# Routing of a mixture of experts moved out of its own stage and into the attention beside it

## The chip, the core and the metric

The kernel runs on one core of a Trainium2 chip. The core has a matrix engine (TensorE, PE), a vector engine (VectorE, DVE), a scalar engine (ScalarE, ACT), a general engine (GpSimd, POOL), and a queue engine (SyncE, SP) that issues nearly all transfers. Each runs its own list of instructions in order and waits for the others at semaphores. Sixteen DMA engines move data. The metric is the device time of one execution in microseconds (us), as the median of several runs.

## What is computed

The input x is 4 sequences of 1024 tokens of 256 values. It is normalised to xn; then attention (16 heads of 16, causal, with a linear position bias) and a mixture of 8 experts, two per token, both read xn, and the output is their sum with x.

```python
xn = _layernorm(x)
x = x + attention(xn, Wq, Wk, Wv, Wo, bo) + moe(xn, router_logits, gating, linear, ...)

# in moe: routing
var = mean(square(xn)); router_input = xn * rsqrt(var + 1e-6) * rsqrt(F) * router_scale
logits = router_input @ router_logits            # 8 per token
probs = softmax(logits)
_, choices = approx_max_k(logits, k=2)
weights = probs / sum(probs of the two chosen)
# tokens sorted by expert, two small matrix products per expert, results put back and weighted
```

## The kernel before, in words

The program is a row of blocks; at the end of a block all engines meet, and nobody starts the next before.

- **project**: 8 chunks of 512 tokens. SP loads a chunk of x (two buffers, `x_in`), DVE takes mean and variance, POOL the inverse deviation, DVE writes `xn`, PE transposes it and multiplies it by the weights of q and k (four quads of heads, `qkpsum`) and of v and the router (`vpsum`). ACT, DVE and POOL split q and k into three bfloat16 parts each (`parts`; L383, L359, L361, L312). SP stores xn, the parts and v, v as four DMAs per chunk (L257). The loop is a hardware loop over pairs of chunks.
- **route**: POOL finishes the scale of the router's input (L490, L492) and writes constants and the causal mask (L494 to L512). DVE runs 58 small dependent instructions, each waiting for the one before (`then`): top two experts per token, softmax weights, and the position ("slot") of each token in a list sorted by expert. In between, PE sums up the counts of tokens per expert (L521, L522) and ACT takes one exponential. Meanwhile SP loads the first three quads of heads (`load_quad`, 13 DMAs each).
- **attend**: 16 steps, one for each quad of heads of each sequence. For every quad there are 19 "items": PE multiplies q and k into `mpsum` (two buffers of 1024 columns, L824), DVE takes the row maxima under the mask (L742); the last item turns the maxima into extra rows of q, which SP writes back with one DMA (L668, `mrow_in`). 26 items are worked off before step 0 (the lead); then a step consists of 18 pairs of heads, with one item of a later step beside each pair (`PAIR_ITEMS`). In a pair PE computes scores (`spsum`, L835), ACT their exponentials (`probs`, L784), POOL masks the diagonal blocks (L722), PE multiplies by v (`cpsum`, L855), and ACT takes the sums away (`ctxT`, L798 and L802, once each per step). The order of all this is written out by hand. In every step POOL also writes four columns of the slot map by indirect DMA, after unit 2 (L712), from small copies that SP fetches a step ahead (L672, L673). SP loads the experts' first weights `w_gu` right after the first maxima rows (L680).
- **experts**: SP loads the finished map into `places` (L936); POOL gathers rows of xn by it (L951); PE, ACT and DVE compute; POOL scatters the results.
- **combine**: output projection and the weighted sum.

## Time and profile before

| | |
|---|---|
| median of 3 runs | 939.3 us (938.69 to 1016.51) |
| profiled execution | 941.12 us, of which the trace spans 939.4 us |
| PE busy | 812.5 us (86%) |
| DVE busy | 562.1 us (60%) |
| ACT busy | 483.2 us (51%) |
| POOL busy | 390.0 us (42%) |

How to read it: "busy" counts instructions that compute. In a timeline row the first number is the start in us from the beginning of the span, the second the time that the merged instructions take, then engine, line, operation, what is written and read; in brackets stands how long the engine was idle before and what ended that. SPq is the issue of a DMA, not its transfer. The granted clock of PE is given as a share of 2.4 GHz. Stages by the timeline: project 0 to 110, route 117.7 to 158, attend 158.5 to 628, experts and combine 632 to 939.

### The profile page before, as it was taken

Reading aid. Unit: us, or ns where it says so; the run is one execution under the profiler, and the core shown is the slowest. Engines: PE = TensorE matmul, PEld = TensorE weight load, DVE = VectorE, ACT = ScalarE, POOL = GpSimd, SP = SyncE. Lnnn points to the kernel's source line nnn. Section 1 sums busy time; section 2 is a strip of 40 time slices with the busy share of each in tenths; the row PEclk is TensorE's granted clock in tenths of the full one; section 3 lists DMA queues with packets and bytes.
Section 4 is the critical chain, followed back from the end, with each engine's and each line's share of the span. In section 5 each row is a group of like instructions: output and inputs, shape, how many; then the busy total and the mean of one; then the engine's idle time right before and its main releaser. Section 6 shows DMA issues by size and latency. Waiting matters only on the chain. (4 is left out here: it accounts for less than half of the span.)

```text
span 939.4 us, 17505 instructions
## 1 busy us (share of the span) xinstructions
PE 812.5 (86%) x5618; PEld 426.3 (45%) x5619; DVE 562.1 (60%) x1560; ACT 483.2 (51%) x1011; POOL 390.0 (42%) x456
## 2 busy tenths in 40 slices
PE   5989601799999999999999999856999999999598
PEld 2555400134444444444444444313555656555497
DVE  4767364988888888888888888301222222222177
ACT  2333300067777777777777777852333333333374
POOL 3545340033223233322323332323666666665398
PEclk9999855589999999999999999996999999999799
DMA  4999899295555666555566600009222222222485
GB/s 157 221 263 269 213 107 121 34 253 74 62 61 57 82 81 81 67 62 61 59 82 81 81 3 3 2 6 321 86 84 84 84 84 84 84 85 78 129 245 182
DMA packets 115004, 100.32 MB, mean 107 GB/s; under 512 B 58172, under 2 KB 95676, under 8 KB 114876
## 3 DMA queue, kind: packets, MB, share of 16 engines
q1 hardware_dynamic: 105976, 80.50, 46.9%
q0 software_dynamic: 8960, 18.95, 6.4%
q8 instruction: 37, 0.61, 0.3%
q14 instruction: 31, 0.25, 0.1%
HBM read 63.89 MB, written 35.00 MB: 105 GB/s over the span
## 5 line engine op out<-in xcount | busy, mean ns | idle before, releaser
L784 ACT ACTIVATE probs<-spsum 128x512 f32<-128x512 f32 x576 | 312.1, 604 | 169.6 <-PE spsum L835 163.8
L742 DVE CUSTOM_DVE_ANT_0 junk<-mpsum,mask 128x128 bf16<-128x128 f32 (+7 forms) x512 | 360.0, 754 | 58.5 <-issue 51.7
L824 PE MATMUL mpsum<-ks,qs 102*128 102x512 bf16 (+3 forms) x768 | 183.5, 343 | 45.9 <-DVE cpsum L731 26.3
L722 POOL TENSOR_SCALAR_AFFINE_SELECT probs<-probs 128x512 f32<-128x512 f32 x128 | 78.8, 634 | 340.8 <-ACT probs L784 340.8
L835 PE MATMUL spsum<-qs,ks 105*128 105x512 bf16 (+3 forms) x768 | 199.2, 329 | 10.6 <-ACT probs L784 8.3
L855 PE MATMUL cpsum<-probs,vs 128*17 128x256 f32 (+2 forms) x2560 | 152.7, 360 | 1.5 <-POOL probs L722 0.8
L1037 PE MATMUL gu<-w_gu,xTs 128*128 x288 | 139.2, 607 | 1.7 <-ACT xTs L981 1.7
L1016 DVE COPY hT<-hp 128x256 f32<-128x256 f32 x72 | 30.6, 425 | 167.8 <-PE hp L1044 100.6
L824 PEld LDWEIGHTS mpsum<-ks,qs 102*128 102x128 bf16 x768 | 69.8, 100 | 122.5 <-DVE maxima L742 39.8
L835 PEld LDWEIGHTS spsum<-qs,ks 105*128 105x128 bf16 x768 | 67.1, 97 | 102.9 <-ACT probs L784 52.9
L956 POOL DMA_INDIRECT expert_rows<-y,places x72 | 70.7, 983 | 72.2 <-ACT y L990 42.2
L855 PEld LDWEIGHTS cpsum<-probs,vs 128*17 128x17 f32 x2560 | 59.8, 97 | 77.4 <-issue 36.4
L951 POOL DMA_INDIRECT rows<-xn_rows,places x72 | 69.3, 962 | 34.9 <-issue 20.7
L985 ACT ACTIVATE gate<-gu 128x256 f32<-128x256 f32 x72 | 27.7, 384 | 100.7 <-issue 64.0
L1050 PE MATMUL yp<-w_down,hT 128*128 x288 | 74.2, 380 | 0.4 <-issue 0.4
L1037 PEld LDWEIGHTS gu<-w_gu,xTs 128*128 128x128 f32 x288 | 52.1, 193 | 45.4 <-issue 38.5
L712 POOL DMA_INDIRECT slot_map<-entries_now,slots x64 | 61.8, 966 | 17.2 <-issue 17.2
L417 PE MATMUL qkpsum<-xT,w_qk 128*128 128x512 f32 x128 | 59.8, 612 | 4.4 <-DVE rest L359 3.3
L1014 DVE TENSOR_TENSOR hid<-gu,gate 128x256 f32<-128x256 f32 x72 | 30.2, 420 | 49.3 <-ACT gate L985 49.3
L1050 PEld LDWEIGHTS yp<-w_down,hT 128*128 128x128 f32 x288 | 49.1, 190 | 4.6 <-issue 0.9
L312 POOL TENSOR_TENSOR parts<-rest,parts 128x512 bf16<-128x512 f32 x32 | 37.0, 1157 | 32.0 <-DVE parts L361 32.0
L990 ACT ACTIVATE y<-yp 128x256 f32<-128x256 f32 x72 | 27.7, 384 | 36.2 <-issue 31.8
(124 smaller groups left out, 698.5 us busy)
## 6 DMA issues: line engine op xcount, KB each, us to landing
qk_parts<-parts SPq DMA_DIRECT2D x32, 384.0 KB, 4.4
qs<-qk_parts SPq DMA_DIRECT2D x96, 128.0 KB
ks<-qk_parts SPq DMA_DIRECT2D x96, 128.0 KB
yk<-expert_rows SPq DMA_DIRECT2D x32, 256.0 KB, 3.1
v_rows<-vt SPq DMA_DIRECT2D x32, 136.0 KB, 4.5
vs<-v_rows SPq DMA_DIRECT2D x16, 272.0 KB, 12.0
x_in<-in_x SPq DMA_DIRECT2D x8, 512.0 KB, 6.3
xn_rows<-xn SPq DMA_DIRECT2D x8, 512.0 KB, 5.8
```

The source lines that it names most:

```text
L417: last = pe.matmul(qkpsum[:, q % 2], w_qk[:, dh, q], xT[:, par, dh], start=dh == 0, stop=dh == DH - 1)
L712: pool.indirect_dma_start(scratch["map"], bass.IndirectOffsetOnAxis(ap=slots[:, par, k, i:i + 1].bitcast(U32), axis=0), entries[:, par, k, ...
L722: pool.affine_select(out=part, in_=part, compare_op=ALU.is_ge, fill=0.0, base=0, pattern=[[0, 4], [1, P]], channel_multiplier=-1).then_inc ...
L742: last = dve.tensor_tensor_reduce(junk[:, slot, c:c + w], mpsum[:, slot, c:c + w], keep["mask"][:, S - w:S], 1.0, 3 * NEG, ALU.add, ALU.ma ...
L784: act.activation(probs[:, u % PRING, h], spsum[:, (4 * u + h) % SRING], ACT.Exp, scale=SCALE).then_inc(exp_done, 1)
L824: last = pe.matmul(mpsum[:, slot, at + c:at + e], qs[hq][0:R_MAX, h, qt * P:(qt + 1) * P], ks[hq][0:R_MAX, h, c:e], start=True, stop=True)
L835: last = pe.matmul(spsum[:, (4 * u + h) % SRING, c:c + w], ks[hq][:, h, kt * P:(kt + 1) * P], qs[hq][:, h, q0:q0 + w], start=True, stop=True)
L855: last = pe.matmul(cpsum[32 * h:32 * h + VW, q0 % CH:q0 % CH + w], vs[hq][:, kt, h], probs[:, u % PRING, h, c:c + w], start=i == 0 and (u, ...
L951: pool.indirect_dma_start(rows[:, s % RR], None, scratch["xn"], bass.IndirectOffsetOnAxis(ap=places[:, s, 0:1].bitcast(U32), axis=0)).then ...
L956: pool.indirect_dma_start(scratch["y"], bass.IndirectOffsetOnAxis(ap=places[:, s, 1:2].bitcast(U32), axis=0), y[:, s % RR], None).then_inc ...
L1037: last = pe.matmul(gu[:, par], xT[:, par, dh], w_gu[:, ds(e * DH + dh, 1)].rearrange("p a c -> p (a c)"), start=dh == 0, stop=dh == DH - 1)
L1050: last = pe.matmul(yp[:, par, 0:D], hT[:, par, dh], w_down[:, ds(e * DH + dh, 1)].rearrange("p a c -> p (a c)"), start=dh == 0, stop=dh == ...
```

## The change

1. The block `route` is gone. The router's scale is finished chunk by chunk in project: POOL gets three more instructions per chunk, and ACT applies the scale as it takes the logits out. The constants and the mask are written by POOL in project, after the first chunk's deviations.
2. 13 routing instructions stand on DVE at the start of attend, then the counts (PE, through a slot of `mpsum`, as a new first item), then the usual items. The other 36 turns of routing stand one behind every second pair of heads: 9 per step, in steps 0 to 3.
3. Project is unrolled, has four buffers for x, stores v with one DMA per chunk (rows of all heads, 1088 bytes), and loads the first quad of heads and the constants of all quads itself. Its buffers lie in the memory of `ctxT`, those of the routing in that of `w_gu`.
4. The slot map is written in steps 6 to 13: two columns beside each of units 2 to 5, straight from `slot` and `entries`, so eight per step. `w_gu` is loaded in step 6. `places` is loaded at the end of attend, when the map's writes have landed.
5. In attend SP loads quad 1 first, then the first maxima rows, then quad 2.

```diff
+EARLY_ROUTE = 13
+MAP_FROM = 6
+MAP_UNITS = (2, 3, 4, 5)
...
-        x_in = sb("x_in", [P, 2, 4, D])
+        x_in = sb("x_in", [P, XR, 4, D])
...
-                for q in range(NQ):
-                    sp.dma_start(scratch["v"][q].rearrange("(t p) w -> p t w", p=P)[:, ds(4 * c, 4), :],
-                                 vt[:, par, :, q].rearrange("p t h w -> p t (h w)")).then_inc(v_stored[par], 16)
+                sp.dma_start(scratch["v"].rearrange("(t p) w -> p t w", p=P)[:, 4 * c:4 * c + 4, :],
+                             vt[:, par].rearrange("p t q h w -> p t (q h w)")).then_inc(v_stored[par], 16)
...
+            for c in range(NC):
+                stores(c, c % 2, c + XR < NC)
+                if c == 2:
+                    sp.wait_ge(parts_stored[0], 16 + 16 * 2)
+                if 2 <= c < 5:
+                    load_rows(sp, scratch, heads, 0, 0, (2 * c - 4, 2 * c - 3))
+                if c == 5:
+                    for i in range(2):
+                        sp.wait_ge(v_stored[i], 16 * 2)
+                    load_values(sp, scratch, heads, 0, 0)
...
-                pool.tensor_tensor(keep["msq"][:, ds(4 * c, 4)], rsq[:, par], mv[:, par, :, 1], ALU.mult).then_inc(pool_step, 1)
+                pool.tensor_tensor(msq[:, par], rsq[:, par], mv[:, par, :, 1], ALU.mult).then_inc(pool_step, 1)
+                pool.wait_ge(pool_step, k + 3)
+                pool.tensor_scalar(msqe[:, par], msq[:, par], RMS_EPS, None, ALU.add).then_inc(pool_step, 1)
+                pool.wait_ge(pool_step, k + 4)
+                pool.tensor_tensor(rms[:, par], msqe[:, par], mhalf[:, 0:4], ALU.pow).then_inc(pool_step, 1)
+                pool.wait_ge(pool_step, k + 5)
+                if c >= 2:
+                    pool.wait_ge(v_taken, 4 * (c - 1) + RING)
+                pool.tensor_scalar(rscaled[:, par], rms[:, par], float(D) ** -0.5, None, ALU.mult).then_inc(rms_ready, 1)
...
-def route(nc, ins, scratch, keep, heads):
...
+                if t == MAP_FROM:
+                    sp.wait_ge(routed, 1)
+                    for e in range(NE):
+                        sp.dma_start(keep["w_gu"][:, e * DH:(e + 1) * DH], ins["w_gu"][:, e * DH:(e + 1) * DH]).then_inc(keep["w_gu_in"], 16)
...
+            sp.wait_ge(entries_out, 16 * 2 * NT)
+            sp.dma_start(keep["places"][:, :, :].rearrange("p s c -> p (s c)"), scratch["map"].rearrange("(p s) c -> p (s c)", p=P)).then_inc(keep["places_in"], 16)
...
-                    if j == LOW_LAST[0]:
-                        map_entries(b, hq)
...
+                    if j in MAP_UNITS and t >= MAP_FROM:
+                        map_entries(NU * t + j, len(MAP_UNITS) * (t - MAP_FROM) + MAP_UNITS.index(j))
...
+            route = routing()
+            for _ in range(EARLY_ROUTE):
+                next(route)
+            count_item()
             for k in range(NI - 1):
                 item(0, 0, k)
...
-                for pair in PAIR_ITEMS:
-                    for j, k in pair:
+                for p in range(PAIRS):
+                    for j, k in PAIR_ITEMS[p]:
                         if has(j):
                             item(t + j, (hq + j) % NQ, k)
+                    if p % 2 == 1:
+                        next(route, None)
```

Three places show how the lists change. In the changed program the routing's tiles carry the name `w_gu` and the buffers of project the name `ctxT`, after the memory that they lie in; its lines are numbered anew (L642 is the old L742).

DVE at the start of attend, before:

```order
L433 UNCONDITIONAL_BRANCH
L728 UNCONDITIONAL_BRANCH
L731 MEMSET cpsum 128x512
L742 ISA junk,maxima<-mpsum,mask 128x1024
L742 ISA maxima 128x1
```

and after the change (rows from the start of attend, the row of the counts and the first items):

```order
L631 MEMSET cpsum 128x512
L675 TENSOR_REDUCE w_gu<-logits 128x32
L677 TENSOR_TENSOR w_gu<-logits,w_gu 128x256
L679 TENSOR_TENSOR w_gu<-w_gu 128x256
L681 TENSOR_REDUCE w_gu<-w_gu 128x32
L683 TENSOR_TENSOR w_gu<-w_gu 128x256
L686 SCALAR_TENSOR_TENSOR w_gu<-w_gu,logits 128x256
...
L691 TENSOR_TENSOR w_gu<-w_gu 128x256
L769 COPY w_gu<-mpsum 128x256 x2
L642 ISA junk,maxima<-mpsum,mask 128x1024
```

Thirteen routing instructions and two copies now stand between the clearing of `cpsum` and the first item.

DVE at the start of step 0 of the changed program, where the remaining routing stands behind every second item:

```order
L642 ISA junk,maxima<-mpsum,mask 128x1024
L642 ISA maxima 128x1
L695 TENSOR_REDUCE w_gu<-w_gu 128x32
L642 ISA junk,maxima<-mpsum,mask 128x896
L642 ISA maxima 128x1
L642 ISA junk,maxima<-mpsum,mask 128x128
L642 ISA maxima 128x1
L642 ISA junk,maxima<-mpsum,mask 128x768
L642 ISA maxima 128x1
L642 ISA junk,maxima<-mpsum,mask 128x256
L642 ISA maxima 128x1
L697 RECIPROCAL w_gu<-w_gu 128x32
```

Before, these items followed each other with nothing between them.

POOL at the start of project in the changed program, from the first chunk's deviations to the second's:

```order
L340 TENSOR_TENSOR ctxT<-ctxT 128x4
L342 TENSOR_SCALAR ctxT<-ctxT 128x4
L344 TENSOR_TENSOR ctxT<-ctxT,mhalf 128x4
L348 TENSOR_SCALAR ctxT<-ctxT 128x4
L364 MEMSET mask 128x1024
L366 AFFINE_SELECT mask<-mask 128x1024
L369 IOTA w_gu 128x8
L370 IOTA w_gu 1x576
L371 MEMSET w_gu 128x256
...
L379 IOTA entries 128x32 x4
L333 TENSOR_SCALAR ctxT<-ctxT 128x4
L335 TENSOR_TENSOR ctxT<-ctxT,mhalf 128x4
```

Before, nothing stood between the first chunk's last instruction (then L299) and the second chunk's first (L292).

## Rows read from the trace of the kernel before

**Rows 1.** Windows: stretch, its length, busy us (x instructions) per engine, PEclk, DMA share, GB/s.

```profile
90.00:110.00 20.00, 19.61 (x67) 11.35 (x65) 10.12 (x19) 8.11 (x23) 9.26 (x8) 1.00 1.01 236
130.00:140.00 10.00, 0.58 (x2) 0.14 (x2) 9.07 (x26) 0.42 (x1) 0.00 (x0) 0.50 1.17 127
150.00:165.00 15.00, 4.81 (x13) 1.27 (x13) 5.17 (x14) 0.00 (x0) 0.00 (x0) 0.50 1.15 124
```

**Rows 2.** Timeline, end of project to the first item of attend.

```profile
110.20 2.14 SPq L257 DMA_DIRECT2D v_rows<-vt  x4
117.71 0.36 SPq L478 DMA_DIRECT2D escale<-in_expert_scale  x1
123.55 0.14 POOL L494 IOTA rank_of<- 128x8 f32 x1
125.57 0.42 DVE L547 TENSOR_REDUCE top<-logit 128x32 f32<-128x256 f32 x1
127.15 1.04 POOL L512 TENSOR_SCALAR_AFFINE_SELECT mask<-mask 128x1024 f32<-128x1024 f32 x1
127.40 1.07 DVE L551 TENSOR_TENSOR chosen<-rank_of,first 128x256 f32<-128x256 f32 x1
131.59 0.42 DVE L558 TENSOR_TENSOR both<-chosen 128x256 bf16<-128x256 f32 x1
132.15 0.42 DVE L561 TENSOR_REDUCE esum<-expd 128x32 f32<-128x256 f32 x1
139.07 0.42 DVE L581 COPY cnt<-counts 128x256 f32<-128x256 f32 x1
148.52 0.18 DVE L604 TENSOR_SCALAR tile_expert<-tile_f 1x72 int32<-1x72 f32 x1
157.29 0.54 SPq L157 DMA_DIRECT2D vs<-v_rows  x1
158.51 0.48 DVE L731 MEMSET cpsum<- 128x512 f32 x1 [9.81 <-DVEq L730]
160.27 1.23 DVE L742 CUSTOM_DVE_ANT_0 junk<-mpsum,mask 128x1024 bf16<-128x1024 f32 x1 [1.27 <-issue]
```

**Rows 3.** Waits: total us, times, longest; SP's queue, and PE in 0 to 112.

```profile
PE qkpsum L417 <- DVE rest L359: 3.3, 4, 1.9
...
SPq L272 <- DMA v_rows<-vt: 4.7, 1, 4.7
```

**Rows 4.** Timeline of project, one late chunk, and POOL in the first.

```profile
14.82 0.23 POOL L292 TENSOR_SCALAR veps<-mv 128x4 f32<-128x4 f32 x1 [5.77 <-DVE mv L334]
15.13 1.04 POOL L294 TENSOR_TENSOR rstd<-veps,mhalf 128x4 f32<-128x4 f32 x1
49.74 1.41 DVE L329 BATCH_NORM_STATS2 stats<-x_in 128x6 f32<-128x256 f32 x4 [1.76 <-DMA x_in<-in_x]
55.36 3.70 PE L417 MATMUL qkpsum<-xT,w_qk 128*128 128x512 f32 x8 [1.93 <-DVE rest L359]
55.84 1.15 POOL L312 TENSOR_TENSOR parts<-rest,parts 128x512 bf16<-128x512 f32 x1 [1.96 <-DVE parts L361]
```

**Rows 5.** Windows: one step of attend, and the lead's end as PE's clock rises.

```profile
229.69:257.21 27.52, 26.18 (x259) 11.77 (x258) 23.55 (x68) 20.32 (x39) 8.78 (x12) 1.00 0.59 71
185.00:190.00 5.00, 3.99 (x13) 1.16 (x12) 4.56 (x16) 0.00 (x0) 0.00 (x0) 0.50 0.44 122
195.00:200.00 5.00, 4.95 (x62) 2.66 (x61) 4.56 (x15) 3.76 (x8) 1.95 (x4) 1.00 1.05 352
```

**Rows 6.** Timeline of ACT, `ctxT` in step 0 and in step 13.

```profile
202.18 0.59 ACT L798 ACTIVATE ctxT<-cpsum 128x512 f32<-128x512 f32 x1
...
559.75 0.59 ACT L798 ACTIVATE ctxT<-cpsum 128x512 f32<-128x512 f32 x1
```

**Rows 7.** Waits in 250 to 550.

```profile
DVE junk L742 <- issue: 37.8, 88, 1.3
```

**Rows 8.** Timeline, end of attend to the first tile of experts.

```profile
627.55 0.60 ACT L802 ACTIVATE ctxT<-cpsum 128x512 f32<-128x512 f32 x1 [2.14 <-PE cpsum L855]
632.45 0.36 SPq L936 DMA_DIRECT2D places<-slot_map  x1
634.58 0.98 POOL L951 DMA_INDIRECT rows<-xn_rows,places  x1 [7.77 <-DMA places<-slot_map]
640.45 0.66 PE L1028 MATMUL tp<-ident,rows 128*128 128x128 f32 x2 [12.96 <-DMA rows<-xn_rows,places]
```

More of the change, by code:

```diff
@@ L16 @@
 from concourse import mybir
+import math
 import numpy as np
@@ L38 @@
 NC = TOK // CH
+XR = 4
 NST = 2 * TOK // P + NE
@@ L161, in project, with load_rows, load_values @@
-def project(nc, ins, scratch, keep):
+def load_rows(sp, scratch, heads, b, hq, products):
+    parts_of = scratch["qk"][hq]
+    for r in products:
+        for side, dst, part in ((0, heads["qs"][hq], Q_PART[r]), (1, heads["ks"][hq], K_PART[r])):
+            src = parts_of[part, 4 * HD * side:4 * HD * (side + 1), S * b:S * (b + 1)]
+            sp.dma_start(dst[HD * r:HD * (r + 1), :, :], src.rearrange("(h d) t -> d h t", d=HD)).then_inc(heads["stack_in"][hq], 16)
+def load_values(sp, scratch, heads, b, hq):
+    sp.dma_start(heads["vs"][hq][:, :, :, :].rearrange("p t h w -> p t (h w)"),
+                 scratch["v"][S * b:S * (b + 1), 4 * VW * hq:4 * VW * (hq + 1)].rearrange("(t p) w -> p t w", p=P)).then_inc(heads["v_in"][hq], 16)
@@ L621, in attend @@
         mparts = sb("mparts", [12 * KT, 2, P], BF16)
-        entries = sb("entries_now", [P, 2, 2, 2, 2], I32)
-        slots = sb("slots", [P, 2, 2, 2], I32)
+        room, early = keep["w_gu_room"], keep["route"]
+        rank_of, tile_no, reset, ones, tri = (early[name] for name in ("rank_of", "tile_no", "reset", "ones", "tri"))
+        logit, escale = keep["logits"][:, :, :], keep["escale"]
+        hit, key, masked_l, expd, prob, picked = (room([P, NT, NE]) for _ in range(6))
+        chosen = [room([P, NT, NE]) for _ in range(2)]
+        cnt, run, pos = (room([P, NE, NT]) for _ in range(3))
+        both = room([P, NT, NE], BF16)
+        counts = [room([P, NT * NE]) for _ in range(2)]
+        past = room([1, NST, NE])
+        first, esum, renorm, guard, sk, slot_f = (room([P, NT]) for _ in range(6))
+        top, pk = ([room([P, NT]) for _ in range(2)] for _ in range(2))
+        slot_i = room([P, 3, NT], I32)
+        total, tiles, ends, base = (room([P, NE]) for _ in range(4))
+        total_i, tiles_i = (room([P, NE], I32) for _ in range(2))
+        tile_f = room([1, NST])
         mpsum = ctx.enter_context(nc.psum_tensor("mpsum", [P, 2, S], F32))
@@ L759, in _, with count_item @@
+            def count_item():
+                n = ITEM_NO[COUNTS]
+                dve.wait_ge(m_taken, n + 1)
+                wait_apart(dve, m_ready, n + 1)
+                for j in range(2):
+                    last = dve.tensor_copy(counts[j], mpsum[:, n % RING, CH * j:CH * j + NT * NE])
+                last.then_inc(m_taken, 1)
+            route = routing()
+            for _ in range(EARLY_ROUTE):
+                next(route)
+            count_item()
             for k in range(NI - 1):
@@ L829, in item, with count_item @@
                     pe.transpose(mpsum[0:4 * KT, slot, 0:P], maxima[:, hq % 2].rearrange("p h q -> p (h q)"), keep["ident"][:, :]).then_inc(m_ready, 1)
+            def count_item():
+                n = ITEM_NO[COUNTS]
+                pe.wait_ge(both_ready, 1)
+                pe.wait_ge(m_taken, n + 1)
+                for j, which in enumerate((tri, ones)):
+                    last = pe.matmul(mpsum[:, n % RING, CH * j:CH * j + NT * NE], which, both,
+                                     start=True, stop=True)
+                last.then_inc(m_ready, 1)
             def scores(n, hq, u, h):
@@ L905, in experts @@
         rows = sb("rows", [P, RR, D])
-        places = sb("places", [P, NST, 2], I32)
+        places, places_in = keep["places"], keep["places_in"]
         xT = sb("xTs", [P, 2, DH, P])
```

404 lines of the change are left out of this document (184 added, 220 removed).

## The prediction

> **What bounds the kernel now.** First the windows by stage [rows 1]. In project PE is busy 19.6 of 20 us at full clock: it is the bound there. Between 110 and 158 us PE does nearly nothing (0.58 us of the ten from 130 to 140), the only busy engine is DVE, and the DMA engines are full (share 1.17) with the loads of three quads. The timeline of that stretch [rows 2] shows two things side by side: DVE's chain of small instructions, from before 125.57 to 148.7 us, and SP's queue, whose last load is issued at 157.8 us; the block ends by the later of the two. So the removal of DVE's chain alone would bring nothing: the loads have to go as well, and the change takes both away. In attend a step lasts 27.5 us and repeats to 0.1 us: thirteen steps take 357.57 us [rows 6]. PE is busy 26.2 us of it, DVE 23.55, ACT 20.3, POOL 8.8 [rows 5]: PE leads, DVE has 4.0 us left, POOL plenty. What ends DVE's idle time are items of PE (shown as "issue"), 88 short waits of 0.43 us in 300 us [rows 7]. At the end of attend 4.3 us pass until SP starts, and 2.1 us more until POOL has the map [rows 8].
>
> **The change, part by part.**
>
> *Project.* (a) Four buffers for x: a late x stopped DVE for 1.76 us and behind it PE for 1.93 us [rows 4]; over all chunks PE lost 3.3 us to such waits [rows 3]. I take all of it as gained: -3.3 (bounds 0 and -3.3). (b) POOL's constants: the first to the end of the mask took 4.6 us (123.55 to 128.19) [rows 2]. The three new instructions cost about what the two of the same kind (0.23 and 1.04 us) and one more small one cost, 1.6 us with their gaps [rows 4]. In the first chunk both stand ahead of the second chunk's deviations, where POOL had 5.77 us idle: 6.2 us into 5.8, and with the semaphore waits between them about 1 us late, which PE pays since q and k of chunk 0 wait behind it on DVE: +1.0 (bounds 0 and 2). In the later chunks the 1.6 us fall into the 1.96 us of idle ahead of POOL's first `parts` [rows 4]: nothing; that cover has 0.3 us to spare. (c) v in one DMA: SP spent 2.14 us on issuing four [rows 2], one takes about 0.5: -1.6 at the end, where the block waits for it. The landing wait of 4.7 us [rows 3] I keep (bounds -2 and 0: fewer packets, or none gained, since the parts stored before it are ahead in the queue). The loads of quad 0 and the constants use SP and the DMA engines beside PE's work, in a stage at share 1.01 [rows 1]: nothing, as long as x comes four chunks ahead.
>
> So SP meets the others 3.9 us earlier than 117.04 us (its wait ends 4.7 us after the issue at 112.34), and DVE, which started 0.7 us after SP's last issue at the other block end (157.83, 158.51), starts at 113.8.
>
> *Start of attend.* Clearing `cpsum` 0.5 us. Thirteen routing instructions: from 125.57 to 132.15 lie thirteen of them, 6.58 us, of which 0.65 us come from one that took 1.07 instead of 0.42 us [rows 2]; without it 0.456 us each, 5.9 us in all. Then PE's two count products and back, an estimate of 1.0 us (nearest row: 1.27 us of idle ahead of the first item, for five larger products, as the upper bound; 0.5 as the lower), and two copies like the one at 139.07, 0.9 us with gaps. The first item starts at 113.8 + 0.5 + 5.9 + 1.0 + 0.9 = 122.1 instead of 160.27 us: **-38.1 us**. Quad 0 lies there already. Quad 1 (1.8 MB; at 127 GB/s [rows 1] 14 us) is needed 18 items, some 22 us at the 1.23 of the first, later. The lead runs at the half clock before [rows 5] and DVE sets its pace; it will again.
>
> *Steps 0 to 3.* The remaining 36 turns took DVE from 132.15 to 148.70, 16.55 us [rows 2], 4.1 per step. A routing instruction between two items also ends their overlap, some 0.08 us each: 4.9 per step. DVE then needs 23.55 + 4.9 = 28.4 us in a step that lasts 27.5. Lower bound: everything is filled in, +0.9 per step; nothing less, since DVE cannot be over 100% busy. Upper bound: no idle time can be used, +4.9 per step, 19.6 in all. I take the lower one, +3.7 in all, because DVE's idle time is spread over the step in short waits for PE [rows 7], two buffers of `mpsum` let PE run ahead meanwhile, and a turn is no longer than one such wait.
>
> *Map, `w_gu`, DMAs.* POOL has 18 us idle per step; eight indirect DMAs at 0.98 us with gaps are 10 us, in units that have no mask but the first: nothing. Steps 0 to 5 lose theirs, which gains nothing either. `w_gu` (4 MB) moves from the lead to step 6, behind that step's maxima rows and ahead of a quad that is used three steps later: nothing. What is late next: the second maxima rows stand in SP's queue behind quads 2 and 3, 28 us of transfer, where `w_gu` and quad 3 stood; they are needed a step after these are issued, so at worst some 3 us, once.
>
> *Handover.* `places` is there when experts starts, and POOL gathers at 632.45 instead of 634.58 us [rows 8]: -2.1 (bounds -1 and -4, since the gather then also runs ahead of the weights). Experts and combine are untouched.
>
> **Sum:** -38.1 + 3.7 - 2.1 = **-36.5 us**. The profiled execution goes from 941.12 to 904.6 us, its span from 939.4 to 902.9. It stood 1.8 us above the median; on the median of 939.3 the forecast is **903 us**.
>
> **The rivals.** *DVE becomes the bound for good (0.09).* The turns add to every step in full, because a late item stops PE and PE then stops the scores. For it: with them DVE is the fuller engine. Against it: the two buffers. 19.6 instead of 3.7: 919 us.
>
> *The mask and the routing collide (0.05).* The one row of 1.07 us ran just while POOL's mask instruction (127.15, 1.04 us) was running, and ended 0.28 us after it; its neighbours of the same form took 0.42 [rows 2]. In steps 0 to 3 POOL has eight masks per step, and some 20 of the 36 turns have such a form. If all of them meet a mask, they cost 20 x 0.65 = 13 us: 916 us. Masks cover less than a fifth of a step, so I expect few. This is what the Trainium skill says in "SBUF — State Buffer", section "Who interferes with whom": a DVE instruction with two SBUF inputs contends with a GpSimd instruction that reads SBUF, and the second to come waits for the whole of the other. By that rule, the row agrees, and it speaks against putting the routing beside the masks.
>
> *POOL's chain hurts every chunk (0.05).* If the 1.6 us are not covered, eight chunks cost 13 us: 916 us. The 1.96 us of idle speak against it.
>
> *Slower: PE's clock stays at half (0.03).* PE was granted 0.50 through the whole lead, though 80% busy (3.99 of 5 us), and got 1.00 only as the scores filled its time to 4.95 of 5 us [rows 5]. If DVE's turns keep PE less full at the start of step 0, the clock could stay at 1.2 GHz until the routing ends. A step needs up to 2 x 26.2 us of PE then, +24.9 in each of four, 100 in all: 1003 us. [...] Against it: at half clock PE's own work doubles, and fills it.
>
> *A little of everything above, or a smaller gain in project* is in the forecast's own share, 0.78: 896 (handover -4, landing -2, routing hidden better than I reckon) to 912.
>
> **The numbers.** The likeliest case gives 903. The range of 896 to 914 holds it and the lower part of the rivals' costs, and leaves out about 0.2. Two per cent, about what a measurement of this kernel tells from no change, is 18.8 us: below 920.5 is faster. The forecast and the three middle rivals lie there, but 919 is close: 0.03 of its chance goes to "same". Faster 0.94, same 0.03, slower 0.03.
>
> **What the changed profile would show.** PE's pause between project and attend shrinks from almost 50 us to about 12. The first item lies at 122 us. The distance of ACT's `ctxT` copies is 28.4 us in steps 0 to 3 and 27.5 after; if it is over 30, DVE's idle time could not be filled. Routing instructions of 0.42 us that take 1 us beside masks show the collision. POOL's `parts` instructions start as late after DVE as before, and project ends 2.3 us sooner. In steps 6 to 13 nothing changes its pace. POOL's first gather comes 4.3 us after attend's last copy. Wrong would be the prediction if the pace of steps 0 to 3 is beyond 29.5, if `mpsum` waits appear behind the maxima rows at the end of step 0, or if the block between project and attend costs more than 0.7 us.

## The result, and the profile after

The changed kernel takes 964.82 us (median of 4 runs, 962.33 to 965.74) beside 940.45 us for the kernel before (4 runs): ratio 1.0254, 95% interval 1.0229 to 1.0279. It is slower by 24 us where 36 us less were forecast. One of the four runs of the kernel before, at 1016.51 us, was a slow one, and the ratio leaves it out. Its profiled execution has a span of 960.6 us, 21.2 more than before, and a mean granted clock of 0.926.

I split the difference of the two spans at marks that both traces have: the first item, the copy of the lower half of `ctxT` once a step (L798 before, L819 now, called "the copy" from here on), the last copy of attend, and the first `xTs` of experts.

| stretch | before, us | after, us | difference | forecast |
|---|---|---|---|---|
| start to first item | 160.27 | 120.15 | -40.1 | -38.1 |
| first item to copy 0 | 41.9 | 42.0 | +0.1 | 0 |
| copy 0 to copy 4 (steps 0 to 3) | 110.07 | 116.84 | +6.8 | +3.7 |
| copy 4 to copy 6 | 54.94 | 54.13 | -0.8 | 0 |
| copy 6 to copy 14 (the map's steps) | 220.08 | 280.95 | **+60.9** | 0 |
| copy 14 to last copy | 40.28 | 38.68 | -1.6 | 0 |
| last copy to first `xTs` | 13.59 | 11.98 | -1.6 | -2.1 |
| the rest | 298.3 | 295.9 | -2.4 | 0 |

The start went as worked out. Timeline of the changed kernel, end of project to the first item; it answers to [rows 2]:

```profile
108.20 0.36 SPq L290 DMA_DIRECT2D v_rows<-ctxT  x1
111.87 0.33 SPq L165 DMA_DIRECT2D qs<-qk_parts  x1
112.14 0.48 DVE L631 MEMSET cpsum<- 128x512 f32 x1 [6.37 <-PEq L196]
...
118.52 0.59 PE L858 MATMUL mpsum<-w_gu 128*128 128x256 bf16 x2 [10.92 <-DVE w_gu L691]
...
119.25 0.76 DVE L769 COPY w_gu<-mpsum 128x256 f32<-128x256 f32 x2 [0.98 <-issue]
120.15 1.23 DVE L642 CUSTOM_DVE_ANT_0 junk<-mpsum,mask 128x1024 bf16<-128x1024 f32 x1
```

The pace up to step 5 went the way worked out, though steps 0 to 3 cost more. Windows from copy to copy, steps 0, 1, 3, 5 and 7, with the columns of [rows 5]:

```profile
162.17:190.40 28.23, 26.65 (x259) 11.54 (x257) 25.82 (x79) 20.51 (x39) 4.95 (x8) 1.00 0.86 103
190.40:219.42 29.02, 27.09 (x259) 11.45 (x257) 26.52 (x82) 20.73 (x39) 4.95 (x8) 1.00 0.57 67
248.37:279.01 30.64, 28.41 (x259) 11.89 (x258) 26.92 (x81) 20.74 (x39) 4.95 (x8) 0.94 0.52 63
306.07:333.14 27.07, 26.00 (x259) 11.77 (x258) 23.55 (x68) 20.45 (x39) 6.01 (x9) 1.00 0.59 72
364.84:401.64 36.80, 30.51 (x259) 12.52 (x258) 23.54 (x68) 20.44 (x39) 12.65 (x16) 0.86 0.49 61
```

Step 5, with no map entry but the first of step 6's, is 0.45 us shorter than a step before, which had four. Step 7, with eight, is 9.7 us longer than step 5, with the same busy time of DVE and ACT: everybody waits, and PE's clock is 0.86. The timeline of step 13 shows where. It is the cleanest of the eight, since no quad is loaded any more (DMA share 0.02):

```profile
578.52 0.98 POOL L612 DMA_INDIRECT slot_map<-entries,slot  x1 [0.16 <-issue]
579.81 0.96 POOL L612 DMA_INDIRECT slot_map<-entries,slot  x1 [0.30 <-issue]
...
581.75 1.49 PE L886 MATMUL cpsum<-probs,vs 128*17 128x256 f32 x24
...
583.17 0.39 PE L866 MATMUL spsum<-qs,ks 105*128 105x512 bf16 x1
583.39 0.60 PE L845 MATMUL mpsum<-ks,qs 102*128 102x512 bf16 x3
...
584.26 0.59 PE L845 MATMUL mpsum<-ks,qs 102*128 102x512 bf16 x2
...
587.40 0.96 POOL L612 DMA_INDIRECT slot_map<-entries,slot  x1 [0.30 <-issue]
590.09 2.06 ACT L803 ACTIVATE probs<-spsum 128x512 f32<-128x512 f32 x4 [7.43 <-remote]
590.28 0.83 DVE L642 CUSTOM_DVE_ANT_0 junk<-mpsum,mask 128x640 bf16<-128x640 f32 x1 [6.90 <-issue]
590.74 0.61 PE L866 MATMUL spsum<-qs,ks 105*128 105x512 bf16 x1 [5.88 <-ACT probs L803]
```

POOL issues eight indirect DMAs 1.27 us apart, with no pause: the waits that stand between the pairs were met long before. PE has issued the scores that ACT waits for at 583.17 and DVE's item at 583.39, but both start only at 590.1, 2.7 us behind the start of the eighth DMA. PE's rows give the issue of a matmul, and their ends are modelled, so they can't say when the work was done. But the trace also keeps the times of semaphore updates; here are PE's for the same seven signals in step 4 and in step 13 (`pv_done`: a product of `probs` and `vs` is done; `s_ready`: scores for ACT; `m_ready`: an item for DVE):

```
                              step 4 (no map)          step 13 (eight entries)
pv_done of units 2, 3         281.80, 282.67           585.00, 590.03
s_ready of unit 5             282.96, 283.61, 283.83   590.07, 590.15, 590.18
m_ready, next two items       283.40, 284.26           590.12, 590.23
product (L886 x24) starts     281.13                   581.75
```

In step 4 the updates come 0.67 to 3.1 us behind the product's start, spread over 2.5 us. In step 13 the first comes at 3.25 us, the second at 8.28, and five more within 0.2 us behind it: less than the matmuls take that they report. So the scores and items had been computed, and their updates were held; whether the product ahead of them was itself done in time can't be read from this. ACT's own update of 582.67 is on time, and only PE's are seen to be late. (The record of updates has gaps: DVE's of 583.38 is not in it.) The waits from copy 6 to copy 14 (total us, times, longest) show it as two groups. In the kernel before DVE's longest wait is 1.3 [rows 7] and ACT's 1.8; "remote" and "issue" stand where the profile shows no releaser:

```profile
DVE junk L642 <- issue: 88.2, 67, 6.9
...
ACT probs L803 <- remote: 56.8, 9, 7.5
```

The stop is paid a second time. Windows in step 7: POOL's run, the stop, and what follows.

```profile
364.00:368.00 4.00, 3.66 (x30) 1.50 (x34) 3.43 (x11) 3.69 (x8) 3.09 (x4) 1.00 1.10 135
368.00:376.00 8.00, 2.45 (x25) 0.89 (x17) 1.43 (x5) 0.69 (x3) 4.36 (x5) 0.95 0.90 101
376.00:384.00 8.00, 7.60 (x43) 2.25 (x43) 5.57 (x18) 3.68 (x7) 0.00 (x0) 0.50 0.01 3
```

Behind the pause PE is granted 0.50 (1.2 GHz instead of 2.4), in this step for 10.2 us from 375.3 on. In the 8 us of the last row it issues 43 matmuls where a step at full clock has 76 in 8 us (259 in 27.07): an estimate of 3.5 us of the step's 9.7. The stretch at 0.50 is not the same in every step: with 6.8 us of it (steps 8, 10, 12) a step takes 34.7 us, with 13.7 (steps 9, 11) 36.9. In steps 4 and 5 the clock stays at 1.00.

### The profile page after: what moved, and what is told of

The parts are those of the page before. It is cut to its first block and busy times, and to the rows that moved or that the text cites. A ratio compares the mean times of both kernels' runs of the same rounds, so it can differ in the third digit from the quotient of the medians.

```text
span 960.6 us, 17184 instructions
## 1 busy us (share of the span) xinstructions
PE 835.0 (87%) x5618; PEld 428.0 (45%) x5619; DVE 557.3 (58%) x1560; ACT 488.3 (51%) x1011; POOL 397.2 (41%) x478
## 5 line engine op out<-in xcount | busy, mean ns | idle before, releaser
L642 DVE CUSTOM_DVE_ANT_0 junk<-mpsum,mask 128x128 bf16<-128x128 f32 (+7 forms) x512 | 360.0, 755 | 111.4 <-issue 95.8
L866 PE MATMUL spsum<-qs,ks 105*128 105x512 bf16 (+3 forms) x768 | 205.3, 338 | 48.8 <-ACT probs L803 43.9
L845 PE MATMUL mpsum<-ks,qs 102*128 102x512 bf16 (+3 forms) x768 | 189.6, 352 | 21.8 <-DVE maxima L642 21.1
L886 PE MATMUL cpsum<-probs,vs 128*17 128x256 f32 (+2 forms) x2560 | 162.8, 379 | 1.5 <-POOL probs L622 0.8
L1046 DVE COPY hT<-hp 128x256 f32<-128x256 f32 x72 | 30.6, 425 | 165.5 <-PE hp L1074 120.7
L612 POOL DMA_INDIRECT slot_map<-entries,slot x64 | 61.9, 967 | 18.3 <-issue 17.4
L485 PE MATMUL qkpsum<-ctxT 128*128 128x512 f32 x128 | 60.0, 614 | 1.4 <-DVE ctxT L413 1.0
L361 POOL TENSOR_TENSOR ctxT<-ctxT 128x512 bf16<-128x512 f32 x32 | 34.9, 1091 | 19.9 <-DVE ctxT L428 19.3
```

The costliest lines, as they stand in the source:

```text
L485: last = pe.matmul(qkpsum[:, q % 2], w_qk[:, dh, q], xT[:, par, dh], start=dh == 0, stop=dh == DH - 1)
L612: pool.indirect_dma_start(scratch["map"], bass.IndirectOffsetOnAxis(ap=keep["slot"][:, k, i:i + 1].bitcast(U32), axis=0), keep["entries"][ ...
L642: last = dve.tensor_tensor_reduce(junk[:, slot, c:c + w], mpsum[:, slot, c:c + w], keep["mask"][:, S - w:S], 1.0, 3 * NEG, ALU.add, ALU.ma ...
L845: last = pe.matmul(mpsum[:, slot, at + c:at + e], qs[hq][0:R_MAX, h, qt * P:(qt + 1) * P], ks[hq][0:R_MAX, h, c:e], start=True, stop=True)
L866: last = pe.matmul(spsum[:, (4 * u + h) % SRING, c:c + w], ks[hq][:, h, kt * P:(kt + 1) * P], qs[hq][:, h, q0:q0 + w], start=True, stop=True)
L886: last = pe.matmul(cpsum[32 * h:32 * h + VW, q0 % CH:q0 % CH + w], vs[hq][:, kt, h], probs[:, u % PRING, h, c:c + w], start=i == 0 and (u, ...
```

## The experiments

All kernels are the changed one with the edit shown, except e6 and e12, which start from the kernel before. Times are medians; "steps" are distances from copy to copy. The ratios go by runs of the kernel before that were made beside each group: 944.03 us for e1 to e4, 942.50 for e5 to e8, 943.97 for e9 to e12, 939.32 for e13 to e15. Two per cent is taken as the least that counts as a change of the time; the steps in the traces show smaller ones. Theory 1 is "a run of back-to-back indirect DMAs on POOL holds PE's semaphore updates". Its rivals: "each DMA costs, wherever it stands" (2), "only the product of units 2 and 3 is hit" (3), "a busy POOL does it" (4), "the routing or the loads that the change moved do it" (5).

**e1, one entry a unit.**

```diff
-MAP_UNITS = (2, 3, 4, 5)
+MAP_UNITS = (1, 2, 3, 4, 5, 6, 7, 8)
-                wait_apart(pool, exp_done, 4 * n + SRING)
+                wait_apart(pool, exp_done, 4 * n + 4 + SRING)
-                for e in range(2 * part, min(2 * part + 2, 2 * NT)):
+                for e in range(part, part + 1):
```

> One map entry beside each of units 1 to 8 of steps 6 to 13, each issued only when that unit's own exponentials are done (about 3 us apart) instead of eight back to back; still 64 entries, eight a step. Theory 1 (run of issues): what stops the engines is the run of back-to-back indirect DMAs on POOL: TensorE's semaphore updates are held from about the fourth until 2.6 us after the start of the eighth. Then no stop of over 2 us is left, the step from copy to copy (ctxT copy of step t to that of t+1) is 27.0 to 27.6 us in steps 6 to 13 instead of 34.8 to 36.9, and the kernel takes 898 to 905 us. Theory 2 (count): each of the 64 DMAs costs about 1 us wherever it stands: steps of 34 to 36 us, total 960 to 966. Theory 3 (the product of probabilities and values of units 2 and 3 waits for the DMAs issued ahead of it): still a stop there, shorter since only two or three DMAs are ahead of it: steps of 28 to 30, total 907 to 925.

Measured 900.88 us (899.4 to 901.08), 0.9543 of before [0.9511, 0.9574]. The longest DVE wait is back at 0.8 us, and the clock at 1.00 in the map's steps. The same eight DMAs a step, POOL as busy as in the change:

```profile
360.29:387.70 27.41, 26.15 (x259) 11.76 (x258) 23.55 (x68) 20.54 (x39) 12.63 (x16) 1.00 0.64 81
```

Theory 2 is out: 64 of them cost nothing if they stand 2.1 to 6.0 us apart, as in the step shown. And steps 6 to 13 take 217.1 us instead of 280.95: the 64 us are the run's alone.

**e2, two entries a unit, each pair behind its own unit's exponentials.**

```diff
-                wait_apart(pool, exp_done, 4 * n + SRING)
+                wait_apart(pool, exp_done, 4 * n + 4 + SRING)
```

> Two entries beside each of units 2 to 5 as in the change, but each pair waits for the exponentials of its own unit instead of those of the unit before, so that the second pair and the later ones are about 3 us apart. Theory 1 (run of issues): a pair (2.5 us of POOL) with a gap of 0.5 us behind it holds nothing or little, steps of 27.1 to 28.5 us, total 900 to 912; if the pairs close up into a run again the stop is the old one, total 950 to 966. Theory 2 (count): 960 to 966. Theory 3 (place): steps 28 to 33.

Measured 926.79 us (0.9808 [0.9768, 0.9847]). Steps 30.1 to 31.7. The pace did not hold: the exponentials of two units follow each other closely there, so the timeline shows a first pair, a run of four (365.94, 367.20, 368.46, 369.73) 0.8 us behind it, a stop of 4.55 us for ACT, and the last pair at 374.65, behind the stop. The total lies between theory 1's two cases and is none of them, the steps lie in the range of theory 3, and the ratio leaves open whether it is faster by 2%. It speaks against a cost per DMA; between the theories 1 and 3 it does not decide.

**e3, the eight beside unit 3.**

```diff
-MAP_UNITS = (2, 3, 4, 5)
+MAP_UNITS = (3,)
-                for e in range(2 * part, min(2 * part + 2, 2 * NT)):
+                for e in range(8 * part, min(8 * part + 8, 2 * NT)):
```

> All eight entries of a step back to back as in the change, but begun beside unit 3, one unit (about 3 us) later. Theory 1 (run of issues): the first semaphore update of TensorE that is held comes about 3 to 4 us behind the first DMA, so it moves from the product of units 2 and 3 to the scores of unit 5 or the product of unit 4; the stop ends 2.6 us behind the start of the eighth DMA again; total 955 to 970. Theory 3 (place): the product of units 2 and 3 is done before the DMAs come, so the stop is gone or is under 2 us: total 900 to 925.

Measured 962.83 us, but it decides nothing: the wait beside unit 3 is over with the mask of unit 2, so the run began where the change's begins (first DMA 0.16 us behind the mask). It is a second measurement of the change.

**e5, the eight begun behind unit 3's own exponentials.** As e3, and `4 * n + SRING` becomes `4 * n + 4 + SRING`.

> All eight entries of a step back to back, begun only when unit 3's own exponentials are done: some 2 to 3 us later than in the change, and now just behind the product of units 2 and 3 instead of ahead of it. (The run with the burst beside unit 3 had not moved it: its wait was over with the mask of unit 2.) Theory 1 (run of issues): the products of the next units, and the signals behind them, are held instead, until 2.6 us behind the start of the eighth DMA; the stop is as long or longer, steps 34 to 38 us, total 955 to 975. Theory 3 (only the product of units 2 and 3 with issues ahead of it is held): the stop is gone, steps 27 to 29, total 900 to 920.

Measured 960.78 us, steps 32.0 to 36.3 (34 to 38 expected; the first is the one below). In the step of 364.21 the first DMA starts at 366.18 instead of 1.1 us ahead of the copy, and the stop falls into three for ACT:

```profile
370.43 0.60 ACT L803 ACTIVATE probs<-spsum 128x512 f32<-128x512 f32 x1 [3.04 <-PE spsum L866]
...
373.99 0.60 ACT L803 ACTIVATE probs<-spsum 128x512 f32<-128x512 f32 x1 [1.06 <-PE spsum L866]
...
377.64 1.57 ACT L803 ACTIVATE probs<-spsum 128x512 f32<-128x512 f32 x3 [3.05 <-remote]
```

The last one ends 2.61 us behind the start of the eighth DMA (375.03), in another unit's work. The run did not come behind the product of units 2 and 3 as meant: that product is issued at 366.69, 0.5 us behind the first DMA, and its updates come by 370.4. But the next product, issued at 371.41, is reported only at 377.58, and the last wait is in its time. So theory 3, that only units 2 and 3 are hit, is out. The hold begins early, with one or two DMAs issued, and a few updates come through on the way.

**e4, POOL busy with memsets at the change's place, the map two a unit beside units 5 to 8.**

```diff
-MAP_UNITS = (2, 3, 4, 5)
+MAP_UNITS = (5, 6, 7, 8)
+                    if j == 2 and MAP_FROM <= t < MAP_FROM + 8:
+                        wait_apart(pool, exp_done, 4 * (NU * t + j) + SRING)
+                        for m in range(16):
+                            pool.memset(waste[:, :], 0.0).then_inc(wasted, 1)
+                            pool.wait_ge(wasted, 16 * (t - MAP_FROM) + m + 1)
```

> POOL as busy as in the change, at the same place, but with other work: sixteen memsets of 128x512 (about 0.5 us each) into a buffer of their own beside unit 2 of steps 6 to 13; the map entries go two beside each of units 5 to 8, each pair behind its own unit's exponentials. Theory 1 (it is the indirect DMAs): the memsets stop nobody; steps as in the paced run with two entries a unit, total within 8 us of it. Theory 4 (a busy POOL, by memory port or by masks that come late, stops the others): a stop of several us beside the memsets, in the place where the change has it; total 940 to 966.

Measured 919.74 us, steps 29.1 to 30.5. Beside the memsets (362.23 to 371.5 in the step read) the longest wait of ACT is 1.15 us, where step 4 of the changed kernel has 0.93, and at their end its work is 0.35 us behind that of step 4, as much as in e1 at the same place. The other 2.9 us of this step come while the map's DMAs are issued, which the busy POOL had pushed into a run of four (372.41 to 376.22) and two pairs. Theory 4 is out as the cause of the stop. The total is 7.0 us under e2's, inside what theory 1 allowed.

**e6, the kernel before with eight entries back to back in steps 0 to 7.**

```diff
-                    if j == LOW_LAST[0]:
-                        map_entries(b, hq)
+                    if j == LOW_LAST[0] and t < 8:
+                        map_entries(t)
...
+                for i in range(4 * t, 4 * t + 4):
+                    for k in range(2):
+                        pool.indirect_dma_start(scratch["map"], bass.IndirectOffsetOnAxis(ap=keep["slot"][:, k, i:i + 1].bitcast(U32), axis=0),
+                                                keep["entries"][:, k, i, :], None).then_inc(entries_out[0], 16)
```

> The kernel before with nothing changed but the map: eight entries back to back beside unit 2 of steps 0 to 7 and none in steps 8 to 15, instead of four in each step, read straight from the slots and entries. Theory 1 (run of issues): the stop does not need the routing inside the attention; steps of 34 to 37 us in steps 0 to 7 and 27.1 in steps 8 to 15, against 27.5 before: 8 x 8.3 - 8 x 0.4 = 63 us more, total 995 to 1010. Theory 5 (the stop comes from the routing or the loads that the change moved): steps stay under 29, total 935 to 955.

Measured 998.81 us, 1.0597 of before [1.0569, 1.0625]; steps 2 and 9 of it:

```profile
273.58:308.27 34.69, 27.90 (x259) 12.10 (x258) 23.55 (x68) 20.33 (x40) 12.65 (x16) 0.90 0.46 55
512.30:539.37 27.07, 26.01 (x259) 11.77 (x258) 23.55 (x68) 20.44 (x40) 4.95 (x8) 1.00 0.58 71
```

The stop needs nothing of the change but the run of eight. Theory 5 is out.

**e12, the kernel before with one entry a unit in steps 0 to 7.** As e6, with one DMA beside each of units 1 to 8 behind its own exponentials.

> The kernel before with nothing changed but the map: one entry beside each of units 1 to 8 of steps 0 to 7, each behind its own unit's exponentials, read straight from the slots and entries; none in steps 8 to 15. Theory 1 says that runs of four hold TensorE's updates too, for the 0.45 us by which a step with them is longer than one without: 15 steps x 0.45 = 6.8 us less, 931 to 936 us. If the 0.45 us were the loads of the copies of slots and entries, the same time would come out; if it is neither, the time stays at 939 to 943.

Measured 936.86 us (0.9909 [0.9876, 0.9943]), 0.9 us above the range expected, and under the 2% that count as a change. All its steps from copy 0 to copy 14, with and without entries, take 27.06 or 27.07 us, so the kernel before had paid 0.45 us a step to what this run takes out, its runs of four or the loads of the copies, and copy 0 to last copy falls from 425.37 to 417.60 us. (The profiled span fell by less, 3.8 us: the first item came 5.2 us later in that execution.) The trace of the kernel before tells the two apart: in the step of 312.25 ACT is 0.4 us behind step 4 of the changed kernel from 319.5 on and stays so to the end of the step, and the loads are issued only behind that:

```profile
323.26 0.63 SPq L672 DMA_DIRECT2D entries_now<-entries  x1
```

The stop in small can be read in the kernel before, where I had not looked: the fourth DMA starts at 314.96, PE issues the next scores and item at 315.80 and 316.02, and

```profile
317.07 2.06 ACT L784 ACTIVATE probs<-spsum 128x512 f32<-128x512 f32 x4 [1.78 <-PE spsum L835]
317.26 0.82 DVE L742 CUSTOM_DVE_ANT_0 junk<-mpsum,mask 128x640 bf16<-128x640 f32 x1 [1.25 <-issue]
```

where step 4 of the changed kernel, with no DMA, has 0.93 and 0.74.

**e10, sixteen back to back in steps 6 to 9.** `MAP_UNITS = (2,)`, sixteen per part.

> Sixteen entries back to back beside unit 2 of steps 6 to 9 and none later. Theory 1 (run of issues): the stop ends some 2.6 us behind the start of the sixteenth, 8 x 1.27 = 10.1 us later than with eight; with 36 us for a step with eight this gives 45 to 48 us, four times, so 900.9 + 4 x (18 to 21) = 973 to 985. If a stop had a fixed length for a run of any length, four stops instead of eight: 930 to 935.

Measured 968.75 us; the four steps take 44.0 to 44.7, the others 27.1. ACT stands for 10.11 us, does one exponential at 390.85, while the run goes on, and stands for 5.02 more, until 1.06 us behind the sixteenth start. The direction is theory 1's (a stop that grows with the run; one of fixed length would have given 930 to 935), but both times are below its range: at least one update comes through a long run.

**e11, eight plain DMAs on POOL's queue in steps 12 to 15; the map one a unit in steps 4 to 11.**

```diff
+                    if j == 2 and t >= 12:
+                        wait_apart(pool, exp_done, 4 * (NU * t + j) + SRING)
+                        for e in range(8):
+                            m = 8 * (t - 12) + e
+                            pool.dma_start(scratch["plain"][P * m:P * (m + 1), :], keep["entries"][:, e % 2, m, :]).then_inc(plain_out, 16)
```

> One map entry a unit as in the run with one entry a unit, moved to steps 4 to 11, and in steps 12 to 15 eight plain DMAs back to back on POOL's queue beside unit 2 (128 rows of 8 bytes each, from the same entries into a scratch tensor of their own, to fixed addresses instead of gathered ones). The plain DMAs are extra work. If any DMA that POOL issues back to back holds TensorE's updates: steps 12 to 14 take 33 to 37 us instead of 27.1 and the total is 925 to 945. If only the indirect ones do: those steps stay under 28, total 898 to 906.

Measured 903.85 us; steps 12 to 14 take 27.06, 27.07 and 23.51, as without. The eight take POOL 4.37 us, and ACT goes on beside them:

```profile
495.18 4.37 POOL L609 DMA_DIRECT2D plain_rows<-entries  x8
495.99 0.60 ACT L810 ACTIVATE probs<-spsum 128x512 f32<-128x512 f32 x1 [0.28 <-PE spsum L873]
```

They are in the same software queue of the profile as the indirect ones, and eight of either kind move 256 packets of the same sizes, so neither that queue nor its small packets hold anything; the indirect instruction does. The plain run is shorter than the change's, 4.4 us, but about as long as a run of four indirect ones, which cost 0.45 us; here every exponential of steps 12 and 13 starts within 0.02 us of its time in step 4.

**e9, a memset of 128x512 ahead of each of the eight.**

```diff
-MAP_UNITS = (2, 3, 4, 5)
+MAP_UNITS = (2,)
+                for e in range(8 * part, 8 * part + 8):
+                    pool.memset(waste[:, :], 0.0).then_inc(wasted, 1)
+                    pool.wait_ge(wasted, e + 1)
```

> The change's eight entries beside unit 2 in one run, but POOL does a memset of 128x512 (0.52 us) into a buffer of its own ahead of each, so that the indirect DMAs start some 1.9 us apart instead of 1.27. Theory 1a (it is the issue without a pause): TensorE's semaphore updates get through in the pauses; no stop of over 2 us, steps 27.1 to 29, total 901 to 917. Theory 1b (it is the number of DMAs within a stretch, or POOL's queue as a whole): the stop lasts as long as the run, now 15 us, steps of 36 to 42, total over 970.

Measured 896.77 us (895.5 to 898.04), 0.9495 of before [0.9455, 0.9534], under the range of theory 1a. Steps 27.1 to 27.6. Still one row of eight beside one unit, longer than the change's, and the longest wait of ACT is 1.3 us:

```profile
366.07 0.97 POOL L615 DMA_INDIRECT slot_map<-entries,slot  x1 [0.28 <-POOL waste L613]
367.04 0.54 POOL L613 MEMSET waste<- 128x512 f32 x1
367.86 0.97 POOL L615 DMA_INDIRECT slot_map<-entries,slot  x1 [0.28 <-POOL waste L613]
```

The spacing of the starts is 1.79 us instead of 1.27.

**e13, the same with a memset of one element.** `waste[:, 0:1]`.

> As the run with pauses, but the memset ahead of each indirect DMA writes one element a partition (under 0.1 us) instead of 512, so that the DMAs start some 1.4 us apart, with another instruction and its wait between them. If what lets TensorE's updates through is that the memset takes time (POOL away from DMAs for half a us), the stop is back: steps 33 to 37, total 945 to 966. If any other instruction between two indirect DMAs does it: steps 27.1 to 28, total 894 to 903.

Measured 945.32 us, steps 30.6 to 34.1: the stop is back, somewhat under the size expected. The starts are 1.35 us apart:

```profile
370.69 0.11 POOL L613 MEMSET waste<- 128x1 f32 x1
371.08 0.96 POOL L615 DMA_INDIRECT slot_map<-entries,slot  x1 [0.28 <-POOL waste L613]
...
372.99 0.60 ACT L806 ACTIVATE probs<-spsum 128x512 f32<-128x512 f32 x1 [4.56 <-remote]
```

Another instruction between two is not enough; it takes a longer pause. 0.08 us more between two starts took 2 us off a step (33.0 instead of 35.1 us in the mean of eight), 0.52 us more took all 8.

**e14, a memset ahead of the first and the fifth only.**

> As the run with pauses, but the memset of 0.52 us stands only ahead of the first and of the fifth of the eight, so that two runs of four follow each other at 0.8 us. If each run of four holds the updates by itself as in the kernel before, where a step with four took 0.45 us more: steps 27.5 to 28.5, total 898 to 910. If one pause in the middle is not enough and the run counts as one of eight: steps 33 to 37, total 945 to 966.

Measured 938.50 us (8 runs, 933.01 to 945.28; 0.9993 of before), steps 30.9 to 33.6: neither of the two. A pause of 0.8 us in the middle does not make two runs of four out of one of eight (27.5 to 28.5 was expected from the kernel before), but it gives 3.4 us a step back. ACT's stop starts in the first four and lasts 4.92 us, until 377.29.

**e7, all routing ahead of the first item.** On e1:

```diff
             for _ in range(EARLY_ROUTE):
                 next(route)
             count_item()
+            for _ in route:
+                pass
```

> As the run with one entry a unit, but all routing instructions stand ahead of the first maximum and none inside the attention. Working: 36 groups of routing leave steps 0 to 3, which took 116.95 us for four instead of 4 x 27.07 = 108.3, so 8.7 us come back; the first maximum comes later by about 40 instructions at 0.3 to 0.45 us, 14 to 17 us. So if the cost of the interleaving is what the steps show, the kernel is 5 to 9 us slower than with the interleaving: 905 to 911 us. If steps 0 to 3 are slow for another reason (loads, clock), they stay at about 29 and it is 914 to 918 us.

Measured 906.10 us, 5.2 more than e1. Copy 0 comes 16.8 us later and steps 0 to 3 take 108.45 us instead of 116.95. So the interleaving costs 8.5 us and saves 16.8 in the profiled executions; the runs show 5.2 of these 8.3, since what follows attend took 4 us less in e7's profile.

**e8, routing behind every third pair.** On e1:

```diff
-MAP_FROM = 6
+MAP_FROM = 7
-                    if p % 2 == 1:
+                    if p % 3 == 2:
                         next(route, None)
```

> As the run with one entry a unit, but routing stands behind every third pair (six in a step, steps 0 to 5) instead of every second (nine, steps 0 to 3), and the map starts in step 7. If routing costs only what exceeds VectorE's slack (27.1 - 23.6 = 3.5 us a step against 9 x 0.45 = 4.1 or 6 x 0.45 = 2.7), steps 0 to 5 take 27.1 to 27.6 and the kernel gains 5 to 8 us: 893 to 896. If each instruction costs its 0.24 us wherever it stands, the same 8.7 us are spread over six steps: 899 to 903.

Measured 895.15 us (893.83 to 896.66), 0.9494 of before [0.9470, 0.9517]. Step 1, with a row less:

```profile
190.26:217.59 27.33, 26.39 (x259) 11.60 (x257) 24.81 (x77) 20.50 (x40) 4.97 (x8) 1.00 0.58 70
```

Steps 0 to 5 take 166.6 us instead of 171.1 in e1 and 162.4 without routing: the same instructions cost 4.2 us in six steps and 8.7 in four. They cost less where VectorE has more room, though not nothing: steps of 27.1 to 27.6 us were expected and 27.3 to 28.6 measured.

**e15, e8's routing and e9's pauses together.**

> The run with pauses (eight entries beside unit 2, a memset of 0.52 us ahead of each) and the routing behind every third pair together, map in steps 7 to 14. Both were measured alone, at 896.8 and, with one entry a unit, 895.2. The steps from copy to copy should be those of each: 27.3 to 28.6 in steps 0 to 5 and 27.1 to 27.6 later, so the sum is 896.8 - 3.5 (573.2 - 570.1 plus a little) = 893, range 890 to 896. Should the run of pauses cost more where no quad is loaded (step 14), 893 to 898.

Measured 895.54 us (893.99 to 897.23), 0.9533 [0.9512, 0.9555]: inside the range, but no faster than e8, since e1's spread had left no stop for the pauses to remove. e8, e9 and e15 are the fastest kernels of this study, too close to be told apart; e8 needs no memset, so it is the one to keep: the change as it was meant, 47 us under the kernel before (942.50) and 70 under the change.

## Why the prediction was wrong

**The step that failed** is the one on the map: "eight indirect DMAs at 0.98 us with gaps are 10 us, in units that have no mask but the first: nothing". It counted POOL's time, and POOL did have it: e1 and e9 issue the same 64 in the same steps at a cost of about 1 us in all (217.1 and 217.6 us from copy 6 to copy 14, where eight steps without any take 216.5). What it left out is what the instruction does to others while it runs without a pause. Measured: +60.9 us between copies 6 and 14, or 64 against e1. With e1's 64 us off, the change stands near where it was forecast, 900.9 us against 903, in part by luck: in e1's trace the first item comes 2 us earlier than worked out and the steps without runs of four give 5.4 us that the forecast had at nothing, while steps 0 to 3 cost 3.2 us more. The sentence beside it, "steps 0 to 5 lose theirs, which gains nothing either", failed for the same reason, by 0.45 us a step; that was the warning. [rows 7] had the sign in them, among "88 short waits of 0.43 us in 300 us" with 1.3 as the longest. I averaged them. The timeline of the kernel before shows the longest once a step (1.30 us ahead of 262.27, 1.29 ahead of 289.79, 1.25 ahead of 317.26), each time 2.3 us behind the start of the fourth indirect DMA (259.92, 287.45, 314.96). None of the rivals held it: the one on the slower side was PE's clock in steps 0 to 3. The clock did fall, but mainly behind the stops, in steps 6 to 13, for 3.4 to 13.7 us at a time; in steps 0 to 3 it stood at 0.50 for 3.4 us in all.

**The start: right, and larger.** First item at 120.15 instead of 122.1. The last store of project is issued by 108.56 instead of 112.34, 3.8 us earlier, where 3.9 were worked out; its three terms were not measured by themselves. The landing wait that the prediction had kept at 4.7 us [rows 3] was 2.6, with one store instead of four; thirteen routing instructions took 5.7 us (5.9 worked out), the counts 1.0 (1.0) and the copies 0.9 (0.9).

**Steps 0 to 3: the mechanism right, the size wrong.** Worked out: DVE needs 28.4 us in a step and sets the pace, +3.7 in all. Measured +6.8, or 8.5 by e7, since the steps of before carried 0.45 us of map stop each. DVE was busy 25.8 to 26.9 us of 28.2 to 30.6, so its short idle times could be filled only in part; the pace missed the bound of 29.5 that I had named in step 3 alone, where PE waited 1.40 us for DVE until 258.30 and was granted 0.50 for 3.4 us from 259.2 on (0.94 in the mean of the step). e8 shows the other side: with six turns a step instead of nine half of the cost goes.

**The mask and the routing did not collide.** Of the routing instructions of the form 128x256 in steps 0 to 3 one took longer than its twin outside, 0.62 instead of 0.42 us (L741 at 231.46), and no mask ran beside it; it reads the counts in another order now. One with two inputs overlapped a mask of POOL (L715 at 189.00, 0.42 us, beside the masks from 187.93 to 189.16). The Trainium skill's "SBUF — State Buffer", section "Who interferes with whom", has a DVE instruction with two SBUF inputs wait for a GpSimd instruction that reads SBUF and came first; in this trace it did not show, though a single meeting at a mask's end decides little. 

**Handover:** POOL's gather comes 4.9 us behind the end of the last copy, not 4.3, so -1.5 instead of -2.1. **Second maxima rows:** PE never waits for them between copy 0 and copy 6, where up to 3 us were allowed for; its longest wait there is 1.4 us, for DVE.

**What is shown and what is argued.** Shown by e1, e6, e9, e10, e11 and e13: the stop comes from indirect DMAs that POOL issues without a pause, grows with the run, needs nothing else of this change, and is gone at 1.79 us between starts. Shown by the trace: PE's semaphore updates are late, those of the scores and items after the work itself. Why an indirect DMA holds them is open. The rows can't tell: the packets of each DMA in step 13 move 1.5 us behind its start, steadily, so no backlog of packets grows. The Trainium skill's "Perfetto Trace Analysis", section "DMA Instruction — SWDGE (GPSIMD)", says that such a row ends when the descriptors are written, while work of that DMA is still to come. The trace agrees that the row's end is not the end: the eighth ends at 588.36, its packets move from 588.95 to 589.11, and PE's signals come 0.9 us behind those. The spacing at which the stop vanishes lies between 1.35 and 1.79 us. That would fit an instruction that occupies something for longer than its row of 0.96 us, but no run measured that by itself, nor a pause of POOL at idle instead of a memset at that spacing. That the products of `probs` and `vs` are the first to be late each time was seen, not tested. And no run touched the 144 indirect DMAs of experts, of which the first four gathers also start 1.3 us apart (634.58 to 638.37 in the trace of the kernel before).

## What to carry to other kernels

An engine's idle time is not free for every instruction: before moving DMAs into it, look at one period of the timeline for who waits behind those already there, and scale the longest such wait, not the mean. In this kernel the indirect DMAs on POOL beside a busy TensorE belong one at a time, with other work between them or 1.8 us between starts; the same 64 were worth 0 or 64 us. And small instructions of the engine that is second by load cost little only as long as they fit its slack in each step: nine turns a step cost 2.2 us, six cost 0.7.

## What the runs showed of the hardware

Indirect DMAs issued on POOL 1.27 us apart delay TensorE's semaphore updates, for ACT and DVE alike, until up to 2.7 us behind the start of the last: ACT's waits were 1.78 us with four, 7.4 with eight, 10.1 and 5.0 with sixteen, 4.6 with eight at 1.35 us, at most 1.3 at 1.79 us, and 0.93, as without any, with plain DMAs of the same queue. A pause in TensorE's work cost more than itself: in step 7 it lasted 5.6 us, until 375.98, and the granted clock stood at 0.50 for 10.2 us from 375.3 on.
